# The last third of the first layer's bias and relu, moved from VectorE to GpSimd

## The chip, the core and the metric

The kernel runs on one core of one Trainium2 chip. The metric is the time of one execution on the device, in microseconds (us). PE is TensorE, DVE is VectorE, ACT is ScalarE, POOL is GpSimd, SP is the engine that issues most DMAs.

## What is computed

Sixteen images of 48 channels and 64x64 pixels pass through two residual layers. Each layer is a mixer and then a feed-forward with quantised arithmetic:

```
x = x + _L0_conv_ref(_ln_c(x), ...)      # 3x3 depthwise conv + gelu + 1x1, one of 4 experts
t = _to_tokens(x)
t = t + _L0_ffn_ref(_ln_t(t), L0_ffn_W1, L0_ffn_b1, L0_ffn_W2, L0_ffn_b2)
x = _from_tokens(t, x)
x = x + _L1_conv_ref(_ln_c(x), ...)      # DCT, four selective state-space scans, inverse DCT
t = _to_tokens(x)
t = t + _L1_ffn_ref(_ln_t(t), L1_ffn_W1, L1_ffn_b1, L1_ffn_W2, L1_ffn_b2)
x = _from_tokens(t, x)
```

The feed-forward goes from 48 channels to 192 and back. `q_mul` rounds to an 8-bit float (5 exponent bits, 2 of mantissa), `q_acc` to a 16-bit one (5 and 10):

```
def _qlinear(x, W, b):
    y = q_acc(jnp.einsum('bsk,nk->bsn', q_mul(x), q_mul(W)))
    return q_acc(y + q_mul(b))
h = jax.nn.relu(_qlinear(x, W1, b1))
y = _qlinear(h, W2, b2)
```

## The kernel before

Images are worked on in eight pairs. Two images of 48 channels fill 96 partitions, and their 4096 pixels lie along the free dimension. `pair(p, last)` is the body of a hardware loop on every engine: DCT, the scan of 8 units of 12 steps (`scan_stage`, by far the longest part; the convolution of the pair after runs inside it), inverse DCT, and then `stream`. Every engine has its own copy of these functions, in an order written out by hand; semaphores join them. A line `x.wait_ge(sem, n)` makes engine x wait until `sem` has counted to n, and `.then_inc(sem, 1)` counts.

`stream(...)` works through chunks of 512 pixels (`CH`), 8 per pair and kind (`NCH`). Its list `parts` is, for most pairs, 8 chunks `ffn1` (second layer's feed-forward for pair p), 8 chunks `ffn0` (first layer's feed-forward for pair p+1) and 8 chunks `norm` (the normalisation ahead of the convolution for pair p+2). It is a software pipeline: in step t different engines work on different chunks. For a feed-forward chunk the stages are, with the step in which they are done and the lines of the profile of before:

- PE, L538 (t) subtracts the mean over channels by a matmul, ACT L860 (t) squares, PE L531 (t-1) averages the squares, ACT L849 and L854 (t-1) make 1/sqrt by Ln and Exp, DVE L1149 (t-1) multiplies and writes fp8 (`xq8`).
- PE L550 (t-2): the first layer, three matmuls into three PSUM banks. The 384 hidden values of the two images (192 each) are laid out as 3 x 128: image 0's first 128, image 1's first 128, and in the last third the remaining 64 of both. ACT L867 (t-2) copies all three from PSUM to `hf` in f16 (the first rounding), and counts `hf_ready`.
- DVE (t-2): L1170 adds the bias and takes the maximum with zero for the first two thirds of `hf`, L1172 for the last third, which has another bias column; both write f16 to `hr`. DVE L1189 casts all of `hr` to fp8 (`h8`).
- PE L561 (t-3): the second layer, three matmuls into one bank, bank 7. It waits for `h8` and for `yf_ready` of the chunk before, since the bank must have been read.
- DVE L1141 (t-4) copies that bank to `yf` in f16, DVE L1180 (t-4) adds the output bias (`yb`), POOL L1371 (t-4) makes the residual addition into `x` and counts `ffn_done`. SP stores `x` to `out` after `ffn1`.

Within one step of `stream` DVE's order is L1141, L1149, L1170, L1172, L1180, L1189. PE's is L531, L538, L550, L561. ACT's is L849, L854, L860, L867. All buffers between the stages are double. POOL does nothing in these steps but the residual additions, in its function `ffn`. The normalisation chunks behind the 16 feed-forward chunks use the same order without the feed-forward's stages.

Of the kernel before, what the change touches and what calls it, by code (L numbers as in the profile page):

```python
# [17 lines left out]
ALU = mybir.AluOpType  # L18
# [54 lines left out]
def program(nc, a):  # L73
# [6 lines left out]
    def sem(name):  # L80
        return ctx.enter_context(nc.semaphore(name))

    with ctx:
# [157 lines left out]
        hf_ready = sem("hf_ready")  # L241
        hr_ready = sem("hr_ready")
        h8_ready = sem("h8_ready")
        fc2_ready = sem("fc2_ready")
# [104 lines left out]
        def is_ffn(parts, t):  # L349
            return 0 <= t < len(parts) and parts[t] != "norm"  # L350
# [472 lines left out]
        def _(act):  # L823
# [15 lines left out]
            def stream(n0, f0, parts, P):  # L839

                for t in range(len(parts) + 2):
# [19 lines left out]
                    if is_ffn(parts, t - 2):  # L861
# [3 lines left out]
                        if j >= 2:  # L865
                            act.wait_ge(hr_ready, 2 * (f0 + j - 1))
                        act.activation(hf[:, j % 2, :], ps[:, 4:7, :].rearrange("p b n -> p (b n)"),  # L867
# [213 lines left out]
        def _(dve):  # L1081
# [50 lines left out]
            def stream(n0, f0, parts, edged, P):  # L1132

                for t in range(1, len(parts) + 4):
# [28 lines left out]
                    if is_ffn(parts, t - 2):  # L1163
# [4 lines left out]
                        if j >= 2:  # L1168
                            dve.wait_ge(h8_ready, f0 + j - 1)
                        dve.tensor_scalar(hr[:, j % 2, 0:2 * CH], hf[:, j % 2, 0:2 * CH],  # L1170
                                          b1[:, layer, 0:1], 0.0, ALU.add, ALU.max).then_inc(hr_ready, 1)
                        dve.tensor_scalar(hr[:, j % 2, 2 * CH:], hf[:, j % 2, 2 * CH:],  # L1172
                                          b1[:, layer, 1:2], 0.0, ALU.add, ALU.max).then_inc(hr_ready, 1)
                    if is_ffn(parts, t - 4):
# [7 lines left out]
                    if is_ffn(parts, t - 2):  # L1182

                        j = t - 2
                        dve.wait_ge(hr_ready, 2 * (f0 + j + 1))
                        if j >= 2:
# [168 lines left out]
        def _(pool):  # L1355
# [7 lines left out]

            def ffn(layer, f0, stored):

                for j in range(NCH):
                    pool.wait_ge(yb_ready, f0 + j + 1)
                    if layer == 0 and stored is not None:
                        pool.wait_ge(out_stored[j], stored)
                    part = slice(j * CH, (j + 1) * CH)  # L1370
                    pool.tensor_tensor(x[:, part], (x if layer else col)[:, part], yb[:, j % 2, :],  # L1371
                                       ALU.add).then_inc(ffn_done, 1)

            edges()
            for j in range(NCH):
                pool.wait_ge(pwb_ready, j + 1)
                part = slice(j * CH, (j + 1) * CH)
                pool.tensor_tensor(col[:, part], xin[:, part], pwb0[:, j % 2, :], ALU.add).then_inc(xm_ready, 1)
            ffn(0, 0, None)

            def pair(p, last):
# [50 lines left out]
                if not last:  # L1432
                    pool.wait_ge(mo_copied, (p + 1) * 2 * QUADS)
                    edges()
                ffn(1, p * 2 * NCH + NCH, None)
                if not last:
                    ffn(0, (p + 1) * 2 * NCH, (p + 1) * 16)

# [123 lines left out]
```

## Time and profile before

| | us |
|---|---|
| median of 3 runs | 4772.62 |
| lowest and highest | 4768.94, 4777.07 |
| the profiled execution, its own time | 4770.02 |
| the profiled execution, span from first to last instruction | 4768.1 |

The profile shows one execution. The span leaves out 1.9 us around the program. A row of the timeline gives the start from the beginning of the span and the duration, both in us; what stands in square brackets is how long the engine had been idle before and which instruction ended that. An instruction's recorded duration can reach over the start of the next one on its engine, since the engines are pipelined.

### The profile page before, as it was taken

How to read it: one execution, taken by the hardware profiler on the slowest of the kernel's cores; microseconds unless marked ns; L12 is line 12 of the kernel's file. 1: busy time of each engine (PE TensorE's matmuls, PEld its weight loads, DVE VectorE, ACT ScalarE, POOL GpSimd, SP SyncE). 2: the span in 40 equal slices, each digit the busy share in tenths (PEclk: the TensorE clock that was granted, in tenths of full speed). 3: DMA queues.
4: the chain of work that ended last, by engine and by line, in shares of the span. 5: the costliest groups of instructions: out<-in, count | busy, mean ns of one | idle time of the engine just before them, and what ended most of it. 6: DMA issues, size and time to landing. Idle time of an engine off the chain costs nothing.

```text
span 4768.1 us, 49162 instructions
## 1 busy us (share of the span) xinstructions
PE 4072.2 (85%) x14248; PEld 1478.0 (31%) x14248; DVE 3633.8 (76%) x3157; ACT 2758.8 (58%) x3396; POOL 2337.8 (49%) x1084
## 2 busy tenths in 40 slices
PE   6779986899869998699986998779987799868997
PEld 2322233222332223322243222332233222332223
DVE  1469967699668996589965998659977699667996
ACT  2556646666566665566565664656647566565554
POOL 0137642476316773167631776227742477325663
PEclk9889988899889999799997998979999899887888
DMA  1147641577317762277623775247751576406661
GB/s 39 41 120 173 165 116 42 145 168 175 91 46 169 175 169 64 65 166 176 154 58 86 184 170 141 61 103 171 173 127 42 131 181 164 103 16 150 145 154 48
DMA packets 166829, 580.17 MB, mean 122 GB/s; under 512 B 22460, under 2 KB 23208, under 8 KB 162952
## 3 DMA queue, kind: packets, MB, share of 16 engines
q1 hardware_dynamic: 152168, 538.66, 47.4%
q10 hardware_dynamic: 14336, 37.76, 2.7%
q8 instruction: 132, 2.16, 0.2%
q14 instruction: 193, 1.58, 0.1%
HBM read 467.12 MB, written 71.48 MB: 113 GB/s over the span
## 4 chain that ended last, share of the span: by engine, by line
issue 32%; POOL 29%; PE 20%; ACT 9%; DVE 8%; DMA 1%; POOLq 0%; SPq 0%; ACTq 0%; DVEq 0%
POOL arena L1417 26%; PE ps L531 3%; PE ps L588 3%; ACT arena L867 2%; PE ps L670 2%; PE ps L579 2%; PE ps L735 2%; ACT arena L849 2%; POOL arena L1407 2%; DVE arena L1328 1%; PE ps L716 1%; PE ps L607 1%; POOL x L1425 1%; PE ps L561 1%; ACT arena L860 1%
## 5 line engine op out<-in xcount | busy, mean ns | idle before, releaser
L1417 POOL TENSOR_TENSOR arena<-arena 128x1024 f32<-128x1024 f32 x768 | 1859.6, 2421 | 972.1 <-DVE arena L1328 972.1
L1328 DVE TENSOR_TENSOR_SCAN arena<-arena,ps 128x1024 f32<-128x1024 f32 x768 | 1756.1, 2287 | 102.0 <-ACT arena L1020 4.5
L1020 ACT ACTIVATE arena<-arena,a_all 128x1024 f32<-128x1024 f32 x768 | 868.1, 1141 | 415.2 <-DVE arena L1328 277.3
L1323 DVE TENSOR_TENSOR ps<-ps,arena 128x1024 f32<-128x1024 f32 x768 | 930.7, 1212 | 159.1 <-PE ps L718 158.7
L716 PE MATMUL ps<-arena,spread 32*128 32x512 f32 x1536 | 905.0, 676 | 138.1 <-DVE arena L1328 87.3
L718 PE MATMUL ps<-arena,spread 32*128 32x512 f32 x1536 | 891.7, 676 | 0.0
L735 PE MATMUL ps<-arena,gather 128*32 128x512 f32 x3072 | 545.1, 656 | 41.2 <-POOL arena L1417 41.2
L781 PE MATMUL ps<-x 96*96 96x512 f32 x1008 | 498.5, 612 | 0.0
L716 PEld LDWEIGHTS ps<-arena,spread 32*128 32x128 f32 x1536 | 234.9, 191 | 782.0 <-issue 383.6
L670 PE MATMUL ps<-arena,w_in 96*96 96x512 f32 x512 | 322.5, 788 | 65.7 <-DMA arena<-xq 65.7
L1371 POOL TENSOR_TENSOR x<-x,arena 96x512 f32<-96x512 f32 x64 | 113.9, 1780 | 414.6 <-DVE arena L1180 414.6
L981 ACT ACTIVATE arena<-ps 128x512 f32<-128x512 f32 x128 | 76.4, 597 | 300.7 <-PE ps L702 300.7
L531 PE MATMUL ps<-arena,average 96*96 96x512 f32 x400 | 219.9, 632 | 30.8 <-ACT arena L860 30.8
L781 PEld LDWEIGHTS ps<-x 96*96 96x96 f32 x1008 | 143.1, 162 | 332.3 <-issue 332.3
L1305 DVE TENSOR_TENSOR arena<-arena 96x1024 f32<-96x1024 f32 x64 | 76.8, 1199 | 218.1 <-ACT arena L1006 218.1
L735 PEld LDWEIGHTS ps<-arena,gather 128*32 128x32 f32 x3072 | 107.9, 115 | 432.6 <-issue 354.3
L1407 POOL TENSOR_TENSOR arena<-arena 96x1024 f32<-96x1024 f32 x64 | 150.5, 2351 | 164.8 <-DVE arena L1305 164.8
L718 PEld LDWEIGHTS ps<-arena,spread 32*128 32x128 f32 x1536 | 229.8, 191 | 0.0
L1397 POOL MEMSET arena<- 96x6 f32 x8 | 0.8, 101 | 436.6 <-ACT xq L946 436.6
L849 ACT ACTIVATE arena<-ps,eps 96x512 f32<-96x512 f32 x200 | 136.4, 682 | 125.3 <-PE ps L531 125.3
L999 ACT ACTIVATE arena<-ps 96x512 f32<-96x512 f32 x128 | 70.7, 589 | 238.6 <-DVE arena L1313 226.8
L670 PEld LDWEIGHTS ps<-arena,w_in 96*96 96x96 f32 x512 | 103.3, 214 | 279.1 <-issue 210.3
(158 smaller groups left out, 5639.9 us busy)
## 6 DMA issues: line engine op xcount, KB each, us to landing
arena<-dl SPq DMA_DIRECT2D x768, 512.0 KB, 5.7
dl<-arena ACTq DMA_DIRECT2D x64, 384.0 KB, 6.2
x<-pn SPq DMA_DIRECT2D x56, 247.5 KB, 5.9
arena<-in_x SPq DMA_DIRECT2D x9, 1536.0 KB, 9.6
arena<-xq SPq DMA_DIRECT2D x64, 192.0 KB, 7.8
arena<-arena ACTq DMA_DIRECT2D x64, 192.0 KB, 5.6
out<-x SPq DMA_DIRECT2D x64, 192.0 KB, 2.1
arena<-xq SPq DMA_DIRECT2D x64, 191.8 KB, 6.7
```

The source lines that it names most:

```text
L531: pe.matmul(ps[0:R, LN_DEPTH + j % LN_DEPTH, :], average[:], sq[:, j % LN_DEPTH, :], start=True, stop=True).then_inc(averaged, 1)
L670: mm = pe.matmul(ps[0:DI, 6 + c, :], w_in[:, q, j, :], xs[:, i, c * 512 + 2 * j:c * 512 + 2 * j + 512], start=(j == 0), stop=(j == 1))
L716: pe.matmul(ps[:, bank, :], spread[rows[0], r, :], u[rows[0], i, 0:512], start=True, stop=True)
L718: pe.matmul(ps[:, bank + 1, :], spread[rows[1], r, :], u_low[rows[1], i, :], start=True, stop=True).then_inc(ubc_ready, 1)
L735: mm = pe.matmul(ps[b * BLK:(b + 1) * BLK, c, :], gather[:, r, :], hs[:, (r * TRIO + b) % HSS, c * 512:(c + 1) * 512], start=False, stop=( ...
L781: mm = pe.matmul(ps[0:R, 7, :], diag[:, k, :], taps_of(win[:, v % 2], k), start=(k == 0), stop=(k == TAPS - 1), skip_group_check=True)
L849: act.activation(lnv[:, k, :], ps[0:R, LN_DEPTH + k, :], ACT.Ln, bias=eps[0:R, e:e + 1]).then_inc(logged, 1)
L1020: act.activation(da[:, m % DAS, :], dbc[:, m % DBC, :], ACT.Exp, scale=a_all[:, v // 2, m:m + 1]).then_inc(da_ready, 1)
L1323: dve.tensor_tensor(driven, driven, bmat[:, v % 2, :], ALU.mult).then_inc(bu_ready, 1)
L1328: dve.tensor_tensor_scan(hs[:, m % HSS, :], da[:, m % DAS, :], driven, 0.0, ALU.mult, ALU.add).then_inc(h_ready, 1)
L1407: pool.tensor_tensor(u[:, i, :], delta, xi[:, i, :], ALU.mult).then_inc(u_ready, 1)
L1417: pool.tensor_tensor(product, product, cmat[:, v % 2, :], ALU.mult).then_inc(pr_ready, 1)
```

## The change

POOL takes over the last third of bias and relu. The instruction on DVE's line 1172 is taken out, and POOL gets one of the same content ahead of each residual addition. Its completion is counted by a new semaphore, `hr_last`, for which DVE's cast and (two chunks later) ACT's copy into the same buffer wait besides `hr_ready`. POOL's function `ffn` is rewritten as a pipeline over steps t like those of the other engines, and is called once for `ffn1` and `ffn0` together.

```diff
                         act.wait_ge(fc1_ready, f0 + j + 1)
                         if j >= 2:
-                            act.wait_ge(hr_ready, 2 * (f0 + j - 1))
+                            act.wait_ge(hr_ready, f0 + j - 1)
+                            act.wait_ge(hr_last, f0 + j - 1)
...
                         dve.tensor_scalar(hr[:, j % 2, 0:2 * CH], hf[:, j % 2, 0:2 * CH],
                                           b1[:, layer, 0:1], 0.0, ALU.add, ALU.max).then_inc(hr_ready, 1)
-                        dve.tensor_scalar(hr[:, j % 2, 2 * CH:], hf[:, j % 2, 2 * CH:],
-                                          b1[:, layer, 1:2], 0.0, ALU.add, ALU.max).then_inc(hr_ready, 1)
...
-                        dve.wait_ge(hr_ready, 2 * (f0 + j + 1))
+                        dve.wait_ge(hr_ready, f0 + j + 1)
+                        dve.wait_ge(hr_last, f0 + j + 1)
...
-            def ffn(layer, f0, stored):
-
-                for j in range(NCH):
-                    pool.wait_ge(yb_ready, f0 + j + 1)
-                    if layer == 0 and stored is not None:
-                        pool.wait_ge(out_stored[j], stored)
-                    part = slice(j * CH, (j + 1) * CH)
-                    pool.tensor_tensor(x[:, part], (x if layer else col)[:, part], yb[:, j % 2, :],
-                                       ALU.add).then_inc(ffn_done, 1)
+            def ffn(f0, parts, stored):
+
+                for t in range(2, len(parts) + 4):
+                    if is_ffn(parts, t - 2):
+                        j = t - 2
+                        layer = int(parts[j] == "ffn1")
+                        pool.wait_ge(hf_ready, f0 + j + 1)
+                        if j >= 2:
+                            settled(pool)
+                            pool.wait_ge(h8_ready, f0 + j - 1)
+                        settled(pool)
+                        pool.tensor_scalar(hr[:, j % 2, 2 * CH:], hf[:, j % 2, 2 * CH:],
+                                           b1[:, layer, 1:2], 0.0, ALU.add, ALU.max).then_inc(hr_last, 1)
+                    if is_ffn(parts, t - 4):
+                        j = t - 4
+                        layer = int(parts[j] == "ffn1")
+                        pool.wait_ge(yb_ready, f0 + j + 1)
+                        if layer == 0 and stored is not None:
+                            settled(pool)
+                            pool.wait_ge(out_stored[j % NCH], stored)
+                        part = slice(j % NCH * CH, (j % NCH + 1) * CH)
+                        pool.tensor_tensor(x[:, part], (x if layer else col)[:, part], yb[:, j % 2, :],
+                                           ALU.add).then_inc(ffn_done, 1)
...
-                ffn(1, p * 2 * NCH + NCH, None)
-                if not last:
-                    ffn(0, (p + 1) * 2 * NCH, (p + 1) * 16)
+                ffn(p * 2 * NCH + NCH, ("ffn1",) * NCH + (() if last else ("ffn0",) * NCH), (p + 1) * 16)
```

On DVE, in one step of `stream` inside a pair, the order before is this (`arena` holds `hf`, `hr`, `h8`, `yf` and `yb`; `b` is the table of biases; REGISTER_ALU computes a semaphore count):

```order
L1170 TENSOR_SCALAR arena<-arena,b 128x1024 [waits h8_ready,hf_ready]
L1172 TENSOR_SCALAR arena<-arena,b 128x512
L1180 TENSOR_SCALAR arena<-arena,b 96x512 [waits ffn_done,yf_ready]
L1185 REGISTER_ALU
L1189 CAST arena<-arena 128x1536 [waits hr_ready,fc2_ready]
L1141 CAST arena<-ps 96x512 [waits yb_ready,fc2_ready]
L1145 REGISTER_ALU
L1149 TENSOR_TENSOR arena<-ps,arena 96x512 [waits rstd_ready,fc1_ready]
```

And in the changed kernel, where the line numbers have moved by one to two:

```order
L1172 TENSOR_SCALAR arena<-arena,b 128x1024 [waits h8_ready,hf_ready]
L1180 TENSOR_SCALAR arena<-arena,b 96x512 [waits ffn_done,yf_ready]
L1190 CAST arena<-arena 128x1536 [waits fc2_ready,hr_ready,hr_last]
L1143 CAST arena<-ps 96x512 [waits yb_ready,fc2_ready]
L1147 REGISTER_ALU
L1151 TENSOR_TENSOR arena<-ps,arena 96x512 [waits rstd_ready,fc1_ready]
```

The 512-wide instruction has gone, and the cast has one wait more. On POOL, at the start of a run of feed-forward steps inside a pair, there stood only residual additions:

```order
L1367 ISA
L1371 TENSOR_TENSOR x<-x,arena 96x512 [waits yb_ready]
L1367 REGISTER_ALU
L1371 TENSOR_TENSOR x<-x,arena 96x512 [waits yb_ready]
L1367 REGISTER_ALU
```

Now bias and relu of chunk t-2 stand ahead of the residual addition of chunk t-4 (the last two additions of a run follow each other at its end):

```order
L1376 TENSOR_SCALAR arena<-arena,b 128x512 [waits hf_ready]
L1371 REGISTER_ALU
L1376 TENSOR_SCALAR arena<-arena,b 128x512 [waits hf_ready]
L1371 REGISTER_ALU
L1376 TENSOR_SCALAR arena<-arena,b 128x512 [waits hf_ready,h8_ready]
L1386 TENSOR_TENSOR x<-x,arena 96x512 [waits yb_ready]
L1371 REGISTER_ALU
L1376 TENSOR_SCALAR arena<-arena,b 128x512 [waits hf_ready,h8_ready]
L1386 TENSOR_TENSOR x<-x,arena 96x512 [waits yb_ready]
L1371 REGISTER_ALU
```

What moved: POOL has two instructions per step instead of one, and the first waits for ACT's copy, not for DVE.

## Rows read from the trace of the kernel before

**Rows 1.** The page: busy time by engine, and the chain that ended last.

```profile
PE 4072.2 (85%) x14248; PEld 1478.0 (31%) x14248; DVE 3633.8 (76%) x3157; ACT 2758.8 (58%) x3396; POOL 2337.8 (49%) x1084
...
issue 32%; POOL 29%; PE 20%; ACT 9%; DVE 8%; DMA 1%; POOLq 0%; SPq 0%; ACTq 0%; DVEq 0%
POOL arena L1417 26%; PE ps L531 3%; PE ps L588 3%; ACT arena L867 2%; PE ps L670 2%; PE ps L579 2%; PE ps L735 2%; ACT arena L849 2%; POOL arena L1407 2%; DVE arena L1328 1%; PE ps L716 1%; PE ps L607 1%; POOL x L1425 1%; PE ps L561 1%; AC
```

**Rows 2.** Busy time by engine in the 57 us of one run.

```profile
core 0: us, PE busy (x) PEld busy (x) DVE busy (x) ACT busy (x) POOL busy (x), PEclk, DMA share, GB/s
...
706.00:763.00 57.00, 48.08 (x152) 18.73 (x152) 46.16 (x89) 48.42 (x62) 23.41 (x13) 1.00 0.10 29
```

**Rows 3.** Timeline of DVE, two steps: start, us, line, what ended its idling.

```profile
748.22 0.48 DVE L1170 TENSOR_SCALAR arena<-arena,b 128x1024 f16<-128x1024 f16 x1 [0.53 <-ACT arena L867]
748.62 0.35 DVE L1172 TENSOR_SCALAR arena<-arena,b 128x512 f16<-128x512 f16 x1
748.88 0.34 DVE L1180 TENSOR_SCALAR arena<-arena,b 96x512 f16<-96x512 f16 x1
749.15 0.95 DVE L1189 CAST arena<-arena 128x1536 fp8e5<-128x1536 f16 x1
750.01 0.68 DVE L1141 CAST arena<-ps 96x512 f16<-96x512 f32 x1
...
755.71 0.48 DVE L1170 TENSOR_SCALAR arena<-arena,b 128x1024 f16<-128x1024 f16 x1 [0.53 <-ACT arena L867]
```

**Rows 4.** Timeline of all engines: PE and ACT in the same two steps.

```profile
750.79 0.82 PE L561 MATMUL ps<-arena,w 128*96 128x512 fp8e5 x3 [0.42 <-DVE arena L1141]
...
751.45 1.02 PE L531 MATMUL ps<-arena,average 96*96 96x512 f32 x2
...
752.51 0.68 ACT L849 ACTIVATE arena<-ps,eps 96x512 f32<-96x512 f32 x1 [0.45 <-PE ps L531]
...
753.22 0.63 ACT L854 ACTIVATE arena<-arena 96x512 f32<-96x512 f32 x1
753.76 0.57 ACT L860 ACTIVATE arena<-ps 96x512 f32<-96x512 f32 x1
...
754.24 1.44 ACT L867 ACTIVATE arena<-ps 128x1536 f16<-128x1536 f32 x1
```

**Rows 5.** Timeline of POOL in the same two steps.

```profile
749.30 1.80 POOL L1371 TENSOR_TENSOR x<-col,arena 96x512 f32<-96x512 f32 x1 [1.81 <-DVE arena L1180]
```

**Rows 6.** Timeline of DVE and POOL in the last steps of the kernel.

```profile
4757.54 1.80 POOL L1371 TENSOR_TENSOR x<-x,arena 96x512 f32<-96x512 f32 x1 [1.60 <-DVE arena L1180]
...
4758.85 0.77 DVE L1170 TENSOR_SCALAR arena<-arena,b 128x1024 f16<-128x1024 f16 x1
...
4762.25 1.15 POOL L1371 TENSOR_TENSOR x<-x,arena 96x512 f32<-96x512 f32 x1 [0.23 <-DVE arena L1180]
```

**Rows 7.** Timeline of DVE and POOL at one place in the scan.

```profile
899.31 1.20 DVE L1305 TENSOR_TENSOR arena<-arena 96x1024 f32<-96x1024 f32 x1
...
899.47 3.25 POOL L1417 TENSOR_TENSOR arena<-arena 128x1024 f32<-128x1024 f32 x1 [1.39 <-DVE arena L1328]
```

**Rows 8.** POOL's groups by line: count | busy us, mean ns of one | idle before.

```profile
L1407 POOL TENSOR_TENSOR arena<-arena 96x1024 f32<-96x1024 f32 x64 | 150.5, 2351 | 164.8 <-DVE arena L1305 164.8
...
L1425 POOL TENSOR_TENSOR x<-x 96x512 f32<-96x512 f32 x56 | 70.7, 1263 | 0.0
...
L1362 POOL MEMSET arena<- 96x128 f32 x8 | 2.2, 274 | 0.0
```

**Rows 9.** Groups by line, the whole span: the first layer's copy and the removed instruction.

```profile
L867 ACT ACTIVATE arena<-ps 128x1536 f16<-128x1536 f32 x128 | 183.6, 1434 | 1.6 <-PE ps L550 1.6
...
L1172 DVE TENSOR_SCALAR arena<-arena,b 128x512 f16<-128x512 f16 x128 | 44.4, 347 | 0.0
```

More of the change, by code:

```diff
@@ L242, in program @@
         hr_ready = sem("hr_ready")
+        hr_last = sem("hr_last")
         h8_ready = sem("h8_ready")
@@ L1378, in _ @@
                 pool.tensor_tensor(col[:, part], xin[:, part], pwb0[:, j % 2, :], ALU.add).then_inc(xm_ready, 1)
-            ffn(0, 0, None)
+            ffn(0, ("ffn0",) * NCH, None)
             def pair(p, last):
```

## The prediction

> **What bounds the kernel now.** I began with the page. No engine is full: PE is busy 85% of the span, DVE 76%, POOL 49%, and the chain that ended last is spread over waits of 32%, POOL 29% and PE 20%, with the scan's product on line 1417 alone at 26% [rows 1]. The change touches none of that scan, so I looked at the feed-forward steps by themselves. There are 128 of them (the copy on line 867 runs once in each) [rows 9], in nine runs: 8 at the start, 7 runs of 16, 8 at the end. In the 57 us of one run of 16, the reader should see that ACT is busy 48.4 us, PE 48.1, DVE 46.2, POOL 23.4, at a granted clock of 1.00 [rows 2]. Three engines are nearly equal and none is full, so something closes a loop between them.
>
> The timeline shows the loop. DVE starts the first two thirds of bias and relu (line 1170) at 748.22, the last third (1172) at 748.62, the output bias (1180) at 748.88, the fp8 cast (1189) at 749.15 and the next step's copy out of PSUM (1141) at 750.01, over at 750.69 [rows 3]. PE's second layer (561), which waits for that copy, starts at 750.79 and holds back the average (531) to 751.45; ACT goes through 849, 854 and 860 to the copy on line 867 at 754.24, which ends at 755.68 [rows 4], and DVE's next-but-one line 1170 starts at 755.71 [rows 3]. That is 7.49 us for two steps. Two such loops run interleaved, one per parity, so one more microsecond between line 1170 and line 1189 costs half a microsecond per step, or **one microsecond for every two steps: 64 times in the kernel**. (The first steps of a run lack part of the loop, so 64 is a little generous.) I call the distance from 1170 to 1189, now 749.15 - 748.22 = 0.93 us, the gap.
>
> **The change part by part.**
>
> *Removed from DVE:* 128 instructions of 347 ns [rows 9]. They overlap their neighbours, so what one holds is the distance to the next start, 748.88 - 748.62 = 0.26 us. If nothing took their place the gap would be 0.67, and the kernel would gain 64 x 0.26 = 17 us.
>
> *Added to POOL:* the same work, 128 instructions on 128x512 f16, and the cast now waits for it. POOL has room: 23.4 of 57 us. But is it done in time? Two things must be priced.
>
> First, its own length. No row has a POOL tensor_scalar. With two operands, 1024 elements take 2.35 us and 512 take 1.26, so 512 elements cost 1.09 and about 0.17 is fixed [rows 8]. The new instruction reads one operand instead of two; half of 1.09 plus 0.17 is **0.72 us**, which I take. Bound above: the two-operand residual addition, 1.15 us when nothing disturbs it [rows 6]. Bound below: a memset, which reads nothing; 128 elements took 0.27, so 0.10 of it for elements, four times that plus 0.17 is 0.59 [rows 8]. The two operations in one instruction and the per-partition bias speak for the upper side, the 16-bit operand for the lower.
>
> Second, when it may start. The trace shows DVE and POOL shutting each other out. The residual addition beside the cast takes 1.80 us [rows 5] where one alone takes 1.15 [rows 6]: it is 0.65 late, and in effect starts at 749.95, which is 0.15 before the cast's recorded end at 750.10 [rows 3]. The product on line 1417 beside DVE's two-input addition (1305) takes 3.25 instead of 2.35: effective start 900.37, 0.14 before the end of 1305 at 900.51 [rows 7, 8]. It holds the other way round too: a line 1170 that came while POOL was adding took 0.77 instead of 0.49 [rows 3, 6]. Whoever comes first keeps the other out until about 0.15 before its end. Line 1170 starts about 0.03 us after ACT's copy (755.68 to 755.71). POOL follows such a signal later: the residual's start at 749.30 comes 0.08 after the end of line 1180 (748.88 + 0.34) [rows 3, 5]. So DVE is first, and the new instruction begins in effect 0.49 - 0.15 = 0.34 after line 1170 has started.
>
> Sum for the gap: 0.34 (kept out by line 1170) + 0.72 (its length) + 0.08 (signal to DVE, taken as long as the one from DVE to POOL) = 1.14 us against 0.93 now: **+0.21 us**. Line 1180, now the second in DVE's queue, comes while POOL holds the door; it starts in effect 0.15 to 0.2 before POOL's end, runs 0.26, and so does not push the cast by more than a few hundredths. Queued behind the waiting cast on DVE are line 1141, for which PE's second layer waits, and line 1149: they move by the same 0.21, and 1141 is the one on the loop.
>
> 64 x 0.21 = 13.4, rounded **+13 us**. With the bounds: 0.59 gives 64 x 0.08 = +5; 1.15 gives 64 x 0.64 = +41.
>
> *The residual additions* now stand behind the new instruction. They wait for line 1180, whose result comes after POOL's share is done by at least 0.1, so the cast is again ahead of them and they take 1.80 as now. Ending some 1.14 + 0.81 + 1.15 = 3.1 us after line 1170, they are clear of the next one 3.6 to 3.9 us later. In the last steps of a run some chunks of x are finished a few tenths later; the stores of `out` and the normalisation hide that, except for the kernel's last chunk, within the sum's error. The additional wait of ACT's copy (line 867) is for work two steps back and costs nothing: 7 us cover it. So is POOL's wait for the cast two steps back. Nothing in the scan changes, so POOL's 26% there stays.
>
> The Trainium skill speaks against this change: its page "Perfetto Trace Analysis" (section "Optimizing Scalar/DVE Operations") says that moving work between GpSimd and VectorE might not help, since they share a read port that a two-port VectorE instruction holds as an exclusive lock. The lateness of 0.65 and 0.90 us above agrees. Its "GPSIMD Engine Reference" (section "Performance versus the Vector engine") gives about 1.8 cycles per element as the best of a tight loop, 769 ns for 512 elements; no run here shows it. By that figure the sum would be 64 x 0.26 = +17 us.
>
> The profiled execution took 4770.0 us and the sum is made on it: 4770.0 + 13.4 = 4783.4. The median of three is 2.6 higher, 4772.6, and the prediction is for such a median: **4786 us**.
>
> **The rivals.** What this kernel's measurement can tell from no change is 0.2%, 9.5 us, or 0.15 us on the gap.
>
> *A. No difference.* POOL's instruction takes 0.54 to 0.66 us under the lock, or isn't kept out. For it: the memset's 0.59. The gap moves by +0.03 to +0.15 or less: 4773 to 4782. The Trainium skill's "GPSIMD Engine Reference" (section "Engine selection") calls one-input work roughly line-rate on GpSimd; that rule would bring the time here, and no run here shows it.
>
> *B. Faster.* POOL works beside line 1170 without being held, and for less than about 0.5 us; then the gap is its latency of 0.1, plus 0.5, plus 0.08, or DVE's own 0.67, and the gain goes to at most 17 us: 4756. It decides below a gap of 0.78. Against it: every POOL instruction in the trace that came while DVE ran a 1189 or a 1305 was held, and 0.5 is below even the memset's estimate.
>
> *C. The residual slips in front of the cast.* If DVE keeps the door from line 1170 through line 1180, POOL starts its share only after both, at 0.40 + 0.34 - 0.15 = 0.59, and ends at 1.31. The output bias is then long ready, so POOL goes straight on to its residual addition, before DVE has heard of the end, and the cast is shut out for another 1.15 - 0.2 = 0.95. Gap: 1.31 + 0.08 + 0.95 = 2.34, +1.4 us, 64 times: +90 us, 4863. For it: DVE's start-to-start distance of 0.40 is shorter than the 0.49 of line 1170, so the next one is at the door before the first is over. Against it: the door opened at 0.14 to 0.15 before the end in the rows, which is at 0.34, before 0.40, and POOL is already waiting.
>
> *D. POOL's instruction is dear,* 1.0 us or more: +0.49 to +0.64 on the gap and more beyond, 4804 to 4814.
>
> **How the numbers follow.** Forecast (slower by 10 to 30 us) 0.38; A 0.30; B 0.08; C 0.12; D 0.12. Faster by over 0.2%: 0.08. Within 0.2%: A, 0.30. Slower: 0.38 + 0.12 + 0.12 = 0.62. For the range, A and D belong in it, and to leave out no more than 2 in 10 I go from 4764, the lower edge of "same", up to 4863, which just takes in C; B stays out. The forecast's own range is 4778 to 4800.
>
> **What would show it.** In the changed profile: a POOL TENSOR_SCALAR of 128x512 x128, recorded at about 0.9 to 1.0 us (0.72 and the time it is kept out); the cast 1.14 after the first relu line; DVE idle about 0.3 us before the cast, ended by POOL; the output bias of line 1180 lengthened from 0.34 to about 0.9; the residual at 1.80 still; the two-step loop at 7.70. The loop at 7.3 would show B, one near 8.9 with casts of some 1.9 us C. The prediction is wrong if POOL's f16 instruction isn't near 0.72 us alone, or if the lock passes from one to the other in another order than I assumed.

## The result, and the profile after

| | before | changed |
|---|---|---|
| median, us | 4771.7 (4 runs, 4769 to 4777) | 5039.9 (4 runs, 5019 to 5047) |
| ratio | | 1.0553, 95% interval 1.0518 to 1.0588 |
| profiled execution, span, us | 4768.1 | 5043.3 |

The kernel became 5.5% slower, 268 us. I had forecast slower, but by 13 us, and at most 90.

From the page of the changed kernel:

```profile
PE 4209.4 (83%) x14248; PEld 1526.3 (30%) x14248; DVE 3697.3 (73%) x3029; ACT 2767.6 (55%) x3396; POOL 2611.3 (52%) x1212
...
L1376 POOL TENSOR_SCALAR arena<-arena,b 128x512 f16<-128x512 f16 x128 | 312.4, 2440 | 482.2 <-ACT arena L869 481.9
...
L562 PE MATMUL ps<-arena,w 128*96 128x512 fp8e5 x384 | 142.8, 494 | 214.4 <-DVE arena L1143 193.1
L532 PE MATMUL ps<-arena,average 96*96 96x512 f32 x400 | 270.5, 765 | 30.8 <-ACT arena L861 30.8
...
L1190 DVE CAST arena<-arena 128x1536 fp8e5<-128x1536 f16 x128 | 172.4, 1347 | 95.8 <-POOL arena L1376 95.8
```

Against [rows 1] POOL is busy 273 us more, and 312 of its time are in the new instruction, 2.44 us each where I had 0.9 to 1.0 recorded. The cast means 1.35 us, it was 0.95 [rows 3]. PE's second layer and its average have become longer too, with the same matmuls: 494 and 765 ns, where the groups by line of the kernel before have 384 and 632:

```profile
L561 PE MATMUL ps<-arena,w 128*96 128x512 fp8e5 x384 | 105.4, 384 | 80.4 <-DVE arena L1141 74.9 <-DVE arena L1189 5.4
L531 PE MATMUL ps<-arena,average 96*96 96x512 f32 x400 | 219.9, 632 | 30.8 <-ACT arena L860 30.8
```

The windows of the changed kernel over most of one run of 16:

```profile
724.00:808.00 84.00, 60.03 (x148) 23.00 (x147) 50.92 (x70) 48.15 (x63) 53.39 (x27) 0.82 0.07 19
```

The granted clock, 1.00 in [rows 2], is 0.82: for part of the time TensorE ran at 1.2 instead of 2.4 GHz. The timeline of DVE and POOL, a little over one loop of two steps (the new lines: 1172 relu, 1180 output bias, 1190 cast, 1143 copy out of PSUM, 1376 POOL's third, 1386 the residual addition):

```profile
773.29 1.85 DVE L1190 CAST arena<-arena 128x1536 fp8e5<-128x1536 f16 x1 [1.25 <-POOL arena L1376]
774.30 2.89 POOL L1376 TENSOR_SCALAR arena<-arena,b 128x512 f16<-128x512 f16 x1
775.06 0.68 DVE L1143 CAST arena<-ps 96x512 f16<-96x512 f32 x1
775.84 1.44 PE L562 MATMUL ps<-arena,w 128*96 128x512 fp8e5 x3 [3.49 <-DVE arena L1143]
776.26 0.47 DVE L1172 TENSOR_SCALAR arena<-arena,b 128x1024 f16<-128x1024 f16 x1
776.65 0.68 DVE L1180 TENSOR_SCALAR arena<-arena,b 96x512 f16<-96x512 f16 x1
777.07 1.91 PE L532 MATMUL ps<-arena,average 96*96 96x512 f32 x2
777.28 0.96 DVE L1190 CAST arena<-arena 128x1536 fp8e5<-128x1536 f16 x1
...
779.02 0.68 ACT L850 ACTIVATE arena<-ps,eps 96x512 f32<-96x512 f32 x1 [4.98 <-PE ps L532]
...
780.75 1.45 ACT L869 ACTIVATE arena<-ps 128x1536 f16<-128x1536 f32 x1
...
782.23 0.49 DVE L1172 TENSOR_SCALAR arena<-arena,b 128x1024 f16<-128x1024 f16 x1 [1.05 <-ACT arena L869]
...
782.43 2.15 POOL L1376 TENSOR_SCALAR arena<-arena,b 128x512 f16<-128x512 f16 x1 [3.19 <-ACT arena L869]
782.64 0.78 DVE L1180 TENSOR_SCALAR arena<-arena,b 96x512 f16<-96x512 f16 x1
...
784.55 1.15 POOL L1386 TENSOR_TENSOR x<-col,arena 96x512 f32<-96x512 f32 x1
784.67 1.85 DVE L1190 CAST arena<-arena 128x1536 fp8e5<-128x1536 f16 x1 [1.25 <-POOL arena L1376]
```

The loop is the one of [rows 3, 4], cast, copy, second layer, average, ACT, relu, cast. It takes 784.67 - 773.29 = 11.38 us where it took 7.49, and the 3.89 more lie in three places:

- **From the relu to the cast:** 784.67 - 782.23 = 2.44 in place of 0.93, +1.51.
- **From the cast to the copy:** the cast takes 1.85 and the copy starts 1.77 after it (773.29 to 775.06) in place of 0.86, +0.9. The cast of the next loop, at 784.67, is as long, and there the rows show why: POOL's residual addition began at 784.55, 0.12 before it, and shut it out.
- **From the second layer to the average:** 777.07 - 775.84 = 1.23 in place of 0.66, **and from the average to ACT** 1.95 in place of 1.06, +1.46. Nothing was added to PE. It had idled 3.49 us before 775.84, and its matmuls then took 1.44 and 1.91 us in place of 0.82 and 1.02, as at the lower of its two levels of clock.

64 times 3.89 is 249 us. This loop is the commonest length in the trace, and not the only one: counted from one of ACT's copies (line 869) to the next but one, some 45 of the 110 distances inside the runs are 11.2 to 11.4 us, some 45 are 12.3 to 12.7, and the first of each run are shorter. Measured by the starts of the first and the last of ACT's copies in each of the nine runs, subtracted and added up, the feed-forwards took 437 us before and 662 now, +224 (their first steps lack part of the loop). From the last copy of a run to the next scan it is 884 before and 921 now, +36, and the eight scans, 2939 and 2950, differ by no more than they do among kernels whose scans are the same (2926 to 2964 in the kernels below).

### The profile page after: what moved, and what is told of

Read it like the earlier page. It is cut to its first block, busy times and chain, and to the rows that moved or that the text cites. A ratio compares the mean times of both kernels' runs of the same rounds, so it can differ in the third digit from the quotient of the medians.

```text
span 5043.3 us, 49398 instructions
## 1 busy us (share of the span) xinstructions
PE 4209.4 (83%) x14248; PEld 1526.3 (30%) x14248; DVE 3697.3 (73%) x3029; ACT 2767.6 (55%) x3396; POOL 2611.3 (52%) x1212
## 3 DMA queue, kind: packets, MB, share of 16 engines
q14 instruction: 193, 1.58, 0.1%
## 4 chain that ended last, share of the span: by engine, by line
POOL 30%; issue 30%; PE 23%; ACT 8%; DVE 7%; DMA 1%; POOLq 1%; SPq 0%; DVEq 0%; ACTq 0%
POOL arena L1432 25%; PE ps L532 4%; POOL arena L1376 3%; PE ps L589 3%; PE ps L539 2%; PE ps L562 2%; ACT arena L869 2%; PE ps L671 2%; PE ps L736 2%; PE ps L580 2%; POOL arena L1422 1%; DVE arena L1329 1%; PE ps L717 1%; PE ps L608 1%; POOL x L1440 1%
## 5 line engine op out<-in xcount | busy, mean ns | idle before, releaser
L1022 ACT ACTIVATE arena<-arena,a_all 128x1024 f32<-128x1024 f32 x768 | 867.7, 1141 | 418.9 <-DVE arena L1329 275.1
L1376 POOL TENSOR_SCALAR arena<-arena,b 128x512 f16<-128x512 f16 x128 | 312.4, 2440 | 482.2 <-ACT arena L869 481.9
L562 PE MATMUL ps<-arena,w 128*96 128x512 fp8e5 x384 | 142.8, 494 | 214.4 <-DVE arena L1143 193.1
L532 PE MATMUL ps<-arena,average 96*96 96x512 f32 x400 | 270.5, 765 | 30.8 <-ACT arena L861 30.8
L1190 DVE CAST arena<-arena 128x1536 fp8e5<-128x1536 f16 x128 | 172.4, 1347 | 95.8 <-POOL arena L1376 95.8
L1151 DVE TENSOR_TENSOR arena<-ps,arena 96x512 fp8e5<-96x512 f32 x128 | 87.2, 681 | 208.1 <-ACT arena L855 208.1
```

The lines of the kernel that those rows point to most:

```text
L532: pe.matmul(ps[0:R, LN_DEPTH + j % LN_DEPTH, :], average[:], sq[:, j % LN_DEPTH, :], start=True, stop=True).then_inc(averaged, 1)
L562: mm = pe.matmul(ps[0:R, 7, :], w2[:, layer, b, :], h8[:, j % 2, b * CH:(b + 1) * CH], start=(b == 0), stop=(b == 2))
L1022: act.activation(da[:, m % DAS, :], dbc[:, m % DBC, :], ACT.Exp, scale=a_all[:, v // 2, m:m + 1]).then_inc(da_ready, 1)
L1376: pool.tensor_scalar(hr[:, j % 2, 2 * CH:], hf[:, j % 2, 2 * CH:], b1[:, layer, 1:2], 0.0, ALU.add, ALU.max).then_inc(hr_last, 1)
```

## The experiments

### The instruction alone

Eleven forms of POOL instruction, one at a time, ahead of everything else (`price` waits for each to end; some of the lines):

```diff
+            price(pool.memset(f_in, 1.0))
+            bias = b1[:, 0, 1:2]
+            for n in range(2):
+                price(pool.tensor_scalar(h_out[:, 0:512], h_in[:, 0:512], bias, 0.0, ALU.add, ALU.max))
...
+                price(pool.tensor_copy(h_out[:, 0:512], h_in[:, 0:512]))
```

> The kernel before, with eleven kinds of POOL instruction run twice each, one at a time, on idle buffers right behind the set-up (some 25 us are added to the start; nothing else changes). In the changed kernel POOL's bias and relu takes 2.05 to 2.2 us where I had 0.72 from the rows of before. Theory 1, the maximum is what is dear: with add alone 512 elements of f16 take 0.6 to 0.8 us, with the maximum, alone or second, 1.3 or more. Theory 2, two operations in one instruction: add alone and maximum alone both take about 1.0, the two together 2.05. Theory 3, f16 in or out is what is dear: the same instruction on f32 takes under 1.2, and the f16 copy over 1.2. Theory 4, the bias column read per partition: with constants in its place under 1.2. Theory 5, it is not the instruction but the company: run alone it takes about 0.72 here. In all of them the length for 256 and 1024 elements tells the share that goes with the elements; I expect 1.1 and 4.0 us.

Timeline of POOL, the first round:

```profile
26.00 2.00 POOL L1371 TENSOR_SCALAR arena<-arena,b 128x512 f16<-128x512 f16 x1
28.10 1.14 POOL L1372 TENSOR_SCALAR arena<-arena,b 128x256 f16<-128x256 f16 x1
29.33 3.70 POOL L1373 TENSOR_SCALAR arena<-arena,b 128x1024 f16<-128x1024 f16 x1
33.12 1.57 POOL L1374 TENSOR_SCALAR arena<-arena,b 128x512 f16<-128x512 f16 x1
34.78 1.92 POOL L1375 TENSOR_SCALAR arena<-arena 128x512 f16<-128x512 f16 x1
36.79 1.99 POOL L1376 TENSOR_SCALAR arena<-arena,b 128x512 f32<-128x512 f32 x1
...
44.33 1.15 POOL L1379 TENSOR_TENSOR arena<-arena 128x512 f16<-128x512 f16 x1
45.56 1.49 POOL L1380 TENSOR_SCALAR arena<-arena 128x512 f16<-128x512 f16 x1
47.12 0.61 POOL L1381 COPY arena<-arena 128x512 f16<-128x512 f16 x1
```

Alone, with nothing on DVE, the instruction takes 2.00 us (in the second round too): it is not the company (theory 5 falls). With f32 it takes 1.99 and with constants for the bias 1.92, so theories 3 and 4 fall. Add alone (line 1374) takes 1.57, the maximum alone (1380) 1.49, both 2.00. So neither is "the dear one": **a tensor_scalar with one of the two operations costs about 1.5 us for 512 elements, and the second operation 0.4 to 0.5 more.** That is more than the addition of two tensors, 1.15, and 2.5 times a copy, 0.61. 256, 512 and 1024 elements take 1.14, 2.00 and 3.70: about 3.3 ns an element and 0.3 fixed. Reading one tensor instead of two saved nothing. (The whole kernel took 4801 us in its single run; no reading rests on that.)

### Additions held behind the cast

```diff
                         pool.wait_ge(yb_ready, f0 + j + 1)
+                        if is_ffn(parts, t - 2):
+                            settled(pool)
+                            pool.wait_ge(h8_ready, f0 + t - 1)
```

> The changed kernel, but each residual addition on POOL also waits for the cast of the same step, so that it can't come ahead of it. Theory 'slip' (my rival C as the main cost): every second cast takes 1.85 us in place of 0.95 since a residual addition has the shared way into memory; with that gone the kernel gains about 64 x 0.9 = 57 us on the changed one, to some 4985. Theory 'POOL's queue': what closes the loop is POOL's own sequence of bias, addition, bias, 6.1 us from the start of the first to the end of the second; then the cast that is set free is not on the path, the additions start later (behind the cast), and the sequence becomes 2.15 + 0.1 + 0.95 + 0.1 + 1.15 + 2.05 = 6.5 us: the kernel loses 64 x 0.35 = 22 us, to some 5065.

Measured: 1.0418 (1.0381 to 1.0454) over the kernel before, against 1.0553: 1.35 points, 64 us, came back. "Slip" gave 57; "POOL's queue", which I had worked out to a loss of 22, falls. The casts are all 0.96 us in it:

```profile
L1190 DVE CAST arena<-arena 128x1536 fp8e5<-128x1536 f16 x128 | 122.9, 960 | 154.9 <-POOL arena L1376 154.9
```

The nine runs take 600 us, 61 less than in the changed kernel. A wait more on POOL made the kernel faster.

### POOL's instruction without anybody waiting for it

```diff
+                        dve.tensor_scalar(hr[:, j % 2, 2 * CH:], hf[:, j % 2, 2 * CH:],
+                                          b1[:, layer, 1:2], 0.0, ALU.add, ALU.max).then_inc(hr_ready, 1)
...
-                        dve.wait_ge(hr_last, f0 + j + 1)
...
-                        pool.tensor_scalar(hr[:, j % 2, 2 * CH:], hf[:, j % 2, 2 * CH:],
+                        pool.tensor_scalar(spare, hf[:, j % 2, 2 * CH:],
```

> The changed kernel with DVE's instruction for the last third put back, the cast waiting for DVE alone, and POOL's bias and relu written to a buffer that nobody reads (only ACT's copy, two steps later, waits for it to have read its input). So POOL's instruction is there, the wait for it isn't. Theory 'wait': nearly all of the +268 us comes from the cast's waiting; then the time is within 40 us of the kernel before (the lock on the shared way still delays DVE's short instructions by up to 0.4 us, 64 x 0.4 = 26 us). Theory 'POOL is full': bias 2.1 to 2.9 and addition 1.15 to 1.8 us fill a step of 3.75 us, and POOL itself bounds the step at 4.0 to 4.7 us, which gives +30 to +120 us without any wait by DVE.

Measured: 1.0079 (1.0049 to 1.0108), +38 us. The wait makes the most of the 268, as the first theory says; but the 38 were the rival's size too, so the timeline has to tell which of the two it is:

```profile
747.00 0.49 DVE L1173 TENSOR_SCALAR arena<-arena,b 128x1024 f16<-128x1024 f16 x1 [0.69 <-ACT arena L870]
747.20 2.58 POOL L1378 TENSOR_SCALAR arena<-arena,b 128x512 f16<-128x512 f16 x1 [0.50 <-ACT arena L870]
747.40 0.78 DVE L1175 TENSOR_SCALAR arena<-arena,b 128x512 f16<-128x512 f16 x1
...
748.11 0.34 DVE L1183 TENSOR_SCALAR arena<-arena,b 96x512 f16<-96x512 f16 x1
...
748.37 0.95 DVE L1192 CAST arena<-arena 128x1536 fp8e5<-128x1536 f16 x1
...
749.75 1.15 POOL L1388 TENSOR_TENSOR x<-x,arena 96x512 f32<-96x512 f32 x1
```

POOL still idles half a microsecond before its instruction, so it isn't full. DVE's second relu line takes 0.78 in place of 0.35: shut out for 0.44 on the path, and the gap is 748.37 - 747.00 = 1.37 in place of 0.93. The lock costs this much, 64 x 0.44 = 28 of the 38 (the nine runs take 25 us more than before). The reader should also see what did not fit my reading of the lock: the cast started at 748.37 in the middle of POOL's instruction (747.20 to 749.78) and took its usual 0.95. POOL's took 2.58 in place of 2.15; this time it was POOL's that grew.

### A shorter instruction in its place

Two kernels in which POOL does other work on the same third (both leave its bias and relu out): a copy, and an addition of the third to itself.

```diff
-                        pool.tensor_scalar(hr[:, j % 2, 2 * CH:], hf[:, j % 2, 2 * CH:],
-                                           b1[:, layer, 1:2], 0.0, ALU.add, ALU.max).then_inc(hr_last, 1)
+                        pool.tensor_copy(hr[:, j % 2, 2 * CH:], hf[:, j % 2, 2 * CH:]).then_inc(hr_last, 1)
```

> The changed kernel with POOL only copying the last third (bias and relu of it are left out). The copy took 0.61 us alone, near the 0.72 on which my forecast stood, where the real instruction takes 2.00. Theory 'length': the forecast failed by the length of the instruction first, and all that follows (addition ahead of the cast, TensorE's lower clock) comes from it. Then this kernel behaves as forecast: kept out 0.34, own length 0.61, signal 0.09: the gap is 1.04 in place of 0.93, 64 x 0.11 = 7 us, at most 0.4% over the kernel before, casts of 0.95 us, granted clock near 1.00 in the feed-forwards. Theory 'traffic': the third on POOL costs by its semaphores, lock and order whatever its length: 40 us or more.

```diff
+                        pool.tensor_tensor(hr[:, j % 2, 2 * CH:], hf[:, j % 2, 2 * CH:],
+                                           hf[:, j % 2, 2 * CH:], ALU.add).then_inc(hr_last, 1)
```

> The changed kernel with POOL adding the last third to itself (bias and relu of it are left out), which took 1.15 us alone: the upper bound that I had set. If the addition gets ahead of the cast as soon as the output bias (ready at 1.19 + 0.08 = 1.27 us after the first relu line in the changed kernel's trace) is ready before POOL's instruction ends (0.34 + 1.15 = 1.49), then the gap is 1.58 and the cast is shut out for 0.9 more in one or both steps of the loop: 64 x (0.65 + 0.9) = 99 us or more, over 4865. If the addition gets ahead only behind the full length of 2 us, it is 64 x 0.65 = 41 us, about 4812. The clock falls only in the first case.

The copy: 1.0037 (1.0019 to 1.0054), +18 us, inside what I expected (at most 0.4%), and the nine runs take 8 us more than before, where the sum has 7; "traffic" (40 or more) falls. The two operands: 1.0081 (1.0054 to 1.0108), +39 us: my first way, over 99 us, falls, and the size of the second, 41, holds (the nine runs take 31 us more). DVE and POOL in the timeline of the copy, then of the addition:

```profile
747.31 0.49 DVE L1172 TENSOR_SCALAR arena<-arena,b 128x1024 f16<-128x1024 f16 x1 [0.81 <-ACT arena L869]
747.47 0.80 POOL L1376 COPY arena<-arena 128x512 f16<-128x512 f16 x1 [1.15 <-ACT arena L869]
...
748.36 0.96 DVE L1190 CAST arena<-arena 128x1536 fp8e5<-128x1536 f16 x1
...
748.56 1.77 POOL L1385 TENSOR_TENSOR x<-col,arena 96x512 f32<-96x512 f32 x1 [0.29 <-DVE arena L1180]
```

```profile
747.12 0.48 DVE L1172 TENSOR_SCALAR arena<-arena,b 128x1024 f16<-128x1024 f16 x1
...
747.29 1.21 POOL L1376 TENSOR_TENSOR arena<-arena 128x512 f16<-128x512 f16 x1 [0.34 <-ACT arena L869]
747.52 1.13 DVE L1180 TENSOR_SCALAR arena<-arena,b 96x512 f16<-96x512 f16 x1
...
748.59 0.96 DVE L1190 CAST arena<-arena 128x1536 fp8e5<-128x1536 f16 x1
748.79 1.76 POOL L1386 TENSOR_TENSOR x<-col,arena 96x512 f32<-96x512 f32 x1 [0.29 <-DVE arena L1180]
```

The gap is 748.36 - 747.31 = 1.05 and 748.59 - 747.12 = 1.47. My sum of three terms gives 0.34 + 0.61 + 0.09 = 1.04 and 0.34 + 1.15 + 0.09 = 1.58. The addition of two tensors shuts the output bias (line 1180) out until 0.19 before its own end (748.50): line 1180 takes 1.13 in place of 0.34 and ends at 748.65, so it is not ready for POOL's residual addition, and the cast goes first. In the changed kernel bias and relu let line 1180 through early: it took 0.78 and was over 1.16 us before POOL's instruction, and so the residual addition could follow at once. The order therefore hangs on how long POOL's instruction keeps DVE out, and not on its length alone: by length alone the addition of two tensors (over at 1.49, output bias ready at 1.27) would have been enough for the first way.

### TensorE kept at work

```diff
                         mm.then_inc(fc1_ready, 1)
+                        if t % 2 == 1:
+                            for _ in range(3):
+                                pe.matmul(ps[R:128, 7, :], gather[:, 0, :], spread[:].rearrange("p r m -> p (r m)"),
+                                          start=True, stop=True, skip_group_check=True)
```

> The changed kernel with three more f32 matmuls of 128x32 by 128x512 on TensorE in every second feed-forward step, behind the first layer's matmuls, where TensorE idles 3.5 to 3.95 us (64 times; their results go to 32 rows of a PSUM bank that nobody reads). They take 2.6 us at full clock. Theory 'clock': in the changed kernel TensorE's idling has brought the granted clock from 1.00 to 0.80 in the feed-forwards, and on the loop the second layer and the average take 1.23 + 1.95 us in place of 0.66 + 1.06: 1.46 us in 11.4. With the engine kept at work the clock stays at 1.00 and the kernel, with more to do, gets faster by up to 64 x 1.46 = 93 us, to some 4945 to 4960. Rival: the lower clock is not on the path, or the matmuls delay the second layer: the same time or slower than 5040.

Measured: 1.0401 (1.0383 to 1.0418), 4958 us against 5040. A kernel that does 2.8 us more on TensorE 64 times is 1.5% faster. The windows over its run of 16:

```profile
724.00:804.00 80.00, 72.20 (x228) 27.11 (x227) 58.18 (x82) 51.20 (x73) 57.72 (x30) 1.00 0.12 36
```

The clock is back at 1.00. The nine runs take 563 us (662 in the changed kernel), 99 less, where 64 x 1.46 is 93. Two steps take 9.90 us in 85 of the 110 distances between ACT's copies, which is 7.49 + 1.51 + 0.90: the first two places of the list above, without the third.

### The length alone

Both followers taken away: additions behind the cast as above, and one such matmul in every step.

```diff
                         mm.then_inc(fc1_ready, 1)
+                        pe.matmul(ps[R:128, 7, :], gather[:, 0, :], spread[:].rearrange("p r m -> p (r m)"),
+                                  start=True, stop=True, skip_group_check=True)
```

> The changed kernel with the additions held behind the cast and one f32 matmul more (128x32 by 128x512, 0.9 us, its result read by nobody) in every feed-forward step behind the first layer. So the two followers of the long instruction, the addition ahead of the cast and the lower clock, are both taken away, and its length alone is left. Theory: POOL's sequence then sets the step at 4.6 us (bias and relu 2.15, signal 0.1, cast 0.95, signal 0.1, addition 1.15, and some 0.1), 9.2 in place of 7.49 for two: 64 x 1.7 = 110 us over the kernel before, about 4878 (2.3%). Rival: the clock isn't what is left of the 4.2% of that version, or one matmul is too little to hold it: 4930 or more.

Measured: 1.0370 (1.0345 to 1.0395), 4954 us, far from 4878. By the time alone the rival would have it. The trace says that the theory was right where it spoke and silent on the rest: the nine runs take 529 us, 91 over the kernel before, at a clock of 1.00. A step is 4.50 us, which is half of 7.49 + 1.51, and also what POOL's bias and relu (2.15), the wait for the cast (1.20) and the addition (1.15) come to one after another; the runs can't tell which of the two closes it. But the stretches between a run and the next scan take 963 us in place of 884. The windows over one such stretch, of the kernel before and of this one:

```profile
762.00:871.00 109.00, 63.47 (x270) 39.62 (x271) 51.23 (x81) 58.54 (x92) 10.97 (x10) 0.76 0.18 53
```

```profile
791.00:914.00 123.00, 81.40 (x277) 49.17 (x276) 54.22 (x85) 62.21 (x96) 17.06 (x13) 0.65 0.14 41
```

Nearly the same work (277 matmuls and 270) at a clock of 0.65 in place of 0.76. What was won in the feed-forwards was lost behind them in five of the eight stretches (122 to 128 us); the other three took 113 to 114. The added matmuls are not needed for it. With the additions held behind the cast and no matmul added, one stretch of eight is like this (4385 to 4507, 122 us at 0.65), and in the kernel of the next section that has the copy out of PSUM moved as well, four are (122 to 123 us at 0.68). With the matmuls and the additions not held, none is: 111 to 115 us at 0.76 to 0.80. So low a clock came only in kernels with the additions held; why, and why in some stretches alone, these runs don't show.

### The copy out of PSUM first

The loop of [rows 3, 4] pointed to a version of the kernel before: DVE's copy (line 1141) stood behind the cast, and PE's second layer waited for it, while DVE idled mostly 0.5 or 0.8 us before the relu.

```diff
-                    if is_ffn(parts, t - 4):
-                        j = t - 4
+                    if is_ffn(parts, t - 3):
+                        j = t - 3
                         dve.wait_ge(fc2_ready, f0 + j + 1)
                         if j >= 2:
                             dve.wait_ge(yb_ready, f0 + j - 1)
                         dve.tensor_copy(yf[:, j % 2, :], ps[0:R, 7, :]).then_inc(yf_ready, 1)
```

(the block moves from the head of the step to right ahead of the relu)

> The kernel before with one move on DVE: the copy of the second layer's PSUM bank to yf is made in the step in which PE has filled it, ahead of the bias and relu, and no longer behind the next cast. Theory, the two-step loop of 7.49 us runs from ACT's copy over bias, cast and that copy to PE's second layer: the copy then falls into DVE's idle time of 0.5 to 0.8 us before the bias, and the loop goes over the cast's end directly, 0.93 + 0.95 + 0.1 in place of 0.93 + 0.86 + 0.68 + 0.1: 0.59 us less per two steps, 64 x 0.59 = 38 us, to about 4734. Rival: the copy comes too late for the idle time (PE's second layer ends 1.5 us before the next bias at the earliest) and pushes the bias itself by up to 0.6 us: then nothing is gained, 4765 to 4780.

Measured: 0.9944 (0.9925 to 0.9963), 4739 us against 4766: 0.56% faster than the kernel before. The timeline of one step:

```profile
748.06 0.82 PE L561 MATMUL ps<-arena,w 128*96 128x512 fp8e5 x3 [0.29 <-DVE arena L1189]
...
748.91 0.69 DVE L1162 CAST arena<-ps 96x512 f16<-96x512 f32 x1 [0.40 <-PE ps L561]
749.52 0.47 DVE L1170 TENSOR_SCALAR arena<-arena,b 128x1024 f16<-128x1024 f16 x1
...
750.44 0.95 DVE L1189 CAST arena<-arena 128x1536 fp8e5<-128x1536 f16 x1
...
751.53 0.82 PE L561 MATMUL ps<-arena,w 128*96 128x512 fp8e5 x3 [0.29 <-DVE arena L1189]
```

Both the theory and its rival are in it. PE's second layer now waits for the cast itself. But the copy waits for PE and starts the relu at its end, without idling: a loop of one step, 751.53 - 748.06 = 3.47 us in place of 3.75, 128 x 0.27 = 35 us on the runs (437 and 411 us measured, 26).

On the changed kernel with its additions behind the cast the same move left the time of the kernel as it was:

> Both improvements together on the changed kernel: additions held behind the cast (4971 us, 4.2% over the kernel before), and the copy of the second layer's bank ahead of the bias and relu (which gained 0.6% on the kernel before). If the copy's 0.6 us leaves the loop here as well: 64 x 0.6 = 38 us or more with a better clock, to 4900 to 4935, still 3% above the kernel before. If POOL's sequence is what bounds by now (bias 2.15, wait for the cast 1.1, addition 1.15, 4.6 us from start to start), it stays at 4960 to 4975.

1.0427 (1.0408 to 1.0446), against 1.0418 without it. The time is the one of the second case, but the trace has the first case in the feed-forwards. Two of ACT's copies, two steps apart:

```profile
737.95 1.45 ACT L869 ACTIVATE arena<-ps 128x1536 f16<-128x1536 f32 x1
...
747.89 1.45 ACT L869 ACTIVATE arena<-ps 128x1536 f16<-128x1536 f32 x1 [0.18 <-PE ps L551]
```

That is 9.94 us, the commonest length there, where the kernel without the move mostly has 10.5: the copy's 0.6 did leave the loop, and the nine runs take 562 us in place of 600, the 38 that I had expected. POOL's sequence bounds only where the clock had come back to 1.00 (from 768 to the end of that run): there a step is 777.25 - 772.69 = 4.56 us, from one addition to the next. The 38 us were lost elsewhere: the stretches between a run and the next scan take 951 us in place of 928, and the scans 11 more, which is no more than they differ by anyway. One of the four slow stretches:

```profile
1383.00:1505.00 122.00, 75.46 (x272) 45.60 (x271) 51.37 (x80) 60.55 (x93) 13.06 (x11) 0.68 0.18 52
```

And with the output bias moved behind the cast as well:

```diff
+                        dve.tensor_copy(h8[:, j % 2, :], hr[:, j % 2, :], saturate=False).then_inc(h8_ready, 1)
                     if is_ffn(parts, t - 4):
                         j = t - 4
                         layer = int(parts[j] == "ffn1")
                         dve.wait_ge(yf_ready, f0 + j + 1)
...
-                        dve.tensor_copy(h8[:, j % 2, :], hr[:, j % 2, :], saturate=False).then_inc(h8_ready, 1)
```

> The kernel before with the copy of the second layer's bank first (the version that gained 0.56%) and the output bias moved behind the cast as well. In that version a step is one loop of 3.48 us, from the copy over bias, relu, output bias and cast to PE's second layer; the output bias holds 0.26 of it. Without it the cast waits for the second relu line, whose result it reads: 0.40 + 0.35 + 0.10 = 0.85 us behind the first in place of 0.92. Theory: 0.07 us per step, 128 x 0.07 = 9 us less than that version, some 4730 against 4768 of the kernel before (0.8%); POOL's addition no longer runs beside the cast and takes 1.15 us. Rival: the loop is closed elsewhere by then, no gain over 4739.

0.9949 (0.9934 to 0.9965): no gain over 0.9944 that the measurement can tell. The nine runs are 409 us against 411, a third of what I expected.

## Why the prediction was wrong

- **What bounds the steps:** right. The two-step loop was there after the change with every member, and "one microsecond on the gap is 64 us" held where little else changed: the gap grew by 0.12, 0.44 and 0.54 us in the kernels with the copy, the spare buffer and the addition of two tensors, and their nine runs by 8, 25 and 31 us. In the changed kernel 1.51 + 0.9 + 1.46 times 64 is 248, and 224 were measured in the runs.
- **What is removed:** right as far as the rows go: from the first relu line to the output bias it is 0.41 us (782.23 to 782.64), and was 0.66 (748.22 to 748.88). The 17 us that it should give by itself were in no run, and it didn't count.
- **The new instruction's own length, 0.72 us:** this is the term that failed. It takes 2.00. I had no row of a POOL tensor_scalar and took half of a two-operand instruction; worse, I took the undisturbed two-operand addition, 1.15, as the bound above. With 2.00 in the same sum the gap is 0.34 + 2.00 + 0.09 = 2.43, and 2.44 was measured; at 64 us for each microsecond this alone would have been +96, some 4869. Rival D had the dear instruction, but priced it only up to 1.15 us, +41. The figure of the Trainium skill's page "GPSIMD Engine Reference" (section "Performance versus the Vector engine"), 1.8 cycles per element and 769 ns, was no better, and the rule of its section "Engine selection", one-input work at roughly line-rate, holds here for the copy of 0.61 us only.
- **Kept out 0.34 us by the first relu line:** right. POOL's instruction started at 782.43 and took 2.15, 0.15 over its length alone: in effect from 782.58, 0.35 behind the relu at 782.23.
- **"Whoever comes first keeps the other out until about 0.15 before its end":** wrong for this instruction. DVE's output bias, which started at 782.64, was held up 0.44, to 783.08, and POOL's instruction went on to 784.58. A page of the Trainium skill, "SBUF — State Buffer" (section "SBUF: two separate sides"), says much the same as I did, that whoever starts first has the shared pair of ports for the whole instruction; the measurement decides against it for POOL's bias and relu, while the addition of two tensors kept DVE out until 0.19 before its end, as the page would nearly have it. On this rested "the cast is again ahead of the additions". It wasn't: the outcome of rival C came about by a way that I hadn't seen, the output bias being let in early and not ahead of POOL's instruction. Whether a shorter bias and relu would have kept the order, no run shows. The kernels with the shorter instructions show the additions behind the cast, and the one with the additions held back shows the price, 64 us.
- **TensorE's clock:** left out altogether. I read 1.00 in [rows 2] and took PE's 0.66 and 1.06 us as constants. With the longer wait they became 1.23 and 1.95, and with three matmuls put into that wait the clock stood at 1.00 again. In the feed-forwards this is 99 us, as much as the length itself.

The +224 us in the runs are thus: 91 for the length (the kernel under "The length alone"), 99 for the clock (changed kernel against the one with TensorE kept at work), and the remaining 34 for the addition ahead of the cast. This split hangs on the order in which it is made, for the two followers help each other. Holding the additions back took 61 us off the runs with the clock left to itself, and 34 with TensorE kept at work; the added matmuls took off 99 with the additions as they were, and 72 with them held. (The granted clock was 0.84 in most runs of the kernel with additions behind the cast, and 0.78 to 0.82 in the long runs of the changed one.) The 91 are for bias and relu on POOL with the addition behind the cast, since that kernel can't part the instruction's length from POOL's sequence. Of the +36 us between runs and scans part is the end of each run, which has POOL's instruction on its path too, and part the clock, 0.73 to 0.79 there; with TensorE kept at work these stretches took 907, 14 less than in the changed kernel. That the parts can't be simply added up is shown by the kernel with the length alone: with its runs at +91, it still lost 104 elsewhere.

## What to carry to other kernels

An engine with half of its time free is no place for work that another engine waits for in a loop, unless its length there is measured: what counted was the latency, 2.00 us on POOL against the 0.26 that it held of DVE's queue, and not the room. Before such a move, time the exact form by itself; a bound "from the nearest row" of another operation is no bound. And where a stretch stands at full TensorE clock, ask what the clock does if the engine has to wait longer: here it was 99 of the 224 us lost in the feed-forwards. A gain in one stretch has to be looked for in the time of the whole kernel as well: twice here it was gone again in the stretch behind.

## What I had not expected of the hardware

- On GpSimd a tensor_scalar (1.49 to 1.57 us with one operation, 2.00 with two, 512 elements of f16; f32 took the same where it was run) is slower than a tensor_tensor (1.15) and much slower than a copy (0.61).
- The lock between GpSimd and VectorE is not always held for the whole instruction. POOL's bias and relu let a short DVE instruction in 0.5 us after its effective start (in some 55 steps of the changed kernel), and a cast that started in its middle took its usual 0.95 while POOL's grew from 2.15 to 2.58 us. A DVE line 1180 that came near its end (776.65) was held up again, by 0.34.
- More matmuls made a kernel 1.5% faster, by keeping the granted clock of the feed-forwards at 1.00 instead of 0.82; with the residual additions held back as well, the clock was 0.65 instead of 0.76 in most of the stretches behind, which also happened, less often, with no matmul added.
